# A graph network on one core: where the 0/1 matrices of destination lanes are made

## The reference

```
out0 = segment_sum(exp(-edge_weight) * x[src], dst)                  # layer 0
scores = einsum(Q[dst], K[src]) / 4 + edge_attr @ We.T + be          # layer 1, 4 heads
attn = softmax over the edges of a destination;  out = segment_sum(V[src] * attn, dst)
e = leaky_relu(x_l[src] + x_r[dst]) @ att; softmax; segment_sum      # layer 2, one head
h = relu((mean of neighbours + x) @ W1 + b1); the same with W2       # layer 3
```

## Time and profile before

| | us |
|---|---|
| median of three runs | 5168.92 |
| span of the profiled execution, first to last instruction | 3717.5 |
| VectorE busy | 2606.7 (70%) |
| TensorE busy | 2149.9 (58%) |
| POOL busy | 1984.6 (53%) |
| ScalarE busy | 796.1 (21%) |

### The profile page before, as it was taken

The page is one execution under the profiler, slowest core; times in us unless marked ns, Lnnn a source line. Parts: engine busy times, 40 slices in busy tenths (PEclk is TensorE's granted clock), DMA queues, the critical chain, the costliest instruction groups (busy, mean ns, idle before and its releaser), DMA issues. The chain is left out here.

```text
span 3717.5 us, 94213 instructions
## 1 busy us (share of the span) xinstructions
PE 2149.9 (58%) x24555; PEld 1628.6 (44%) x24556; DVE 2606.7 (70%) x5968; ACT 796.1 (21%) x2086; POOL 1984.6 (53%) x1987
## 2 busy tenths in 40 slices
PE   1435777566535555555655553465666666666597
PEld 0225666455534444444544442344444444444232
DVE  3898999888856777776777765477777777777511
ACT  0023555455520111111111110011111111111100
POOL 0112444333327777777777730777777777776000
PEclk9867889756655666666666665566666766666699
DMA  4046777788776667666666630565555555555687
GB/s 148 12 126 170 258 260 261 233 244 237 217 74 184 184 180 190 183 175 183 186 184 182 183 94 9 130 161 146 150 151 144 153 154 148 153 148 147 223 309 282
DMA packets 679457, 646.11 MB, mean 174 GB/s; under 512 B 129015, under 2 KB 513308, under 8 KB 678333
## 3 DMA queue, kind: packets, MB, share of 16 engines
q1 hardware_dynamic: 375773, 346.64, 31.7%
q0 software_dynamic: 77184, 154.07, 17.5%
q10 hardware_dynamic: 226300, 143.41, 12.6%
HBM read 433.64 MB, written 222.40 MB: 176 GB/s over the span
## 5 line engine op out<-in xcount | busy, mean ns | idle before, releaser
L1646 POOL DMA_INDIRECT rows<-nodes_xl,id_slot x832 | 831.1, 999 | 419.3 <-issue 249.5
L1646 POOL DMA_INDIRECT rows<-nodes_kv,id_slot x832 | 825.1, 992 | 290.8 <-issue 244.8
L1842 DVE SCALAR_TENSOR_TENSOR running_counts<-running_counts,same_block,counts_p 128x128 f32<-128x128 f32 x1144 | 393.9, 344 | 412.6 <-PE counts_p L2001 305.7
L2001 PE MATMUL counts_p<-hot_src,hot_blocks 128*128 128x128 bf16 x2288 | 291.9, 281 | 585.8 <-DVE running_counts L1842 584.4
L2001 PEld LDWEIGHTS counts_p<-hot_src,hot_blocks 128*128 128x128 bf16 x2288 | 217.6, 154 | 661.4 <-DVE running_counts L1842 599.4
L2045 PE MATMUL sums<-parts,hot 128*128 128x68 bf16 (+1 forms) x4992 | 325.2, 251 | 250.1 <-DVE parts L1826 250.1
L2045 PEld LDWEIGHTS sums<-parts,hot 128*128 128x128 bf16 x4992 | 311.6, 168 | 271.5 <-issue 271.5
L1091 POOL DMA_INDIRECT msg_by_src<-message,unit_slot x156 | 199.7, 1280 | 311.3 <-DVE message L944 292.4
L1260 PE MATMUL sums<-parts,hot 128*128 128x65 bf16 x3168 | 183.7, 235 | 120.7 <-DVE parts L1237 120.7
L1687 ACT CAST parts<-mixed 128x544 bf16<-128x544 f32 (+1 forms) x208 | 133.0, 639 | 536.1 <-DVE mixed L1810 278.1
L1971 PE MATMUL picked<-rows,ident 128*128 128x512 f32 x208 | 198.2, 1054 | 79.2 <-DMA rows<-nodes_xl,id_slot 68.3
(11 more groups left out here) (490 smaller groups left out, 4289.9 us busy)
## 6 DMA issues: line engine op xcount, KB each, us to landing
hot_src<-hot_src_by_cell SPq DMA_DIRECT2D x1144, 64.0 KB
adjacency<-running_counts ACTq DMA_DIRECT2D x1144, 64.0 KB
hotT<-hotT_by_step SPq DMA_DIRECT2D x208, 256.0 KB
hot<-hot_by_step SPq DMA_DIRECT2D x208, 256.0 KB
blocks<-adjacency SPq DMA_DIRECT2D x40, 1280.0 KB
hot_src_by_cell<-hot POOLq DMA_DIRECT2D x132, 256.0 KB
loc_all<-loc_by_cell SPq DMA_DIRECT2D x104, 256.0 KB
hotT_by_step<-hotT ACTq DMA_DIRECT2D x104, 256.0 KB
```

The costliest lines, as they stand in the source:

```text
L1646: pool.indirect_dma_start(out=rows[:, j, t, :], out_offset=None, in_=table, in_offset=bass.IndirectOffsetOnAxis(ap=ids[:, j, t:t + 1], axis=0)
L1842: v.scalar_tensor_tensor(runs[:, r, q, :], before_it, same[:, bass.ds(J * BBODY + (count_from + q), 1)], counts_p[:, q - HALVES[q >= len(H ...
L2001: ins = nc.tensor.matmul(counts_p[:, q - HALVES[half][0], :], hot_b[:, r, :, t], hot_s[:, r, q, :, g], start=g == 0, stop=g == 1)
```

## The change

`hot` and `hotT` are no longer made in the message stage, stored or loaded. In both attention loops SyncE loads the broadcast lane numbers (`loc_b`, 256 KB a step, ring of four) in the place of the `hotT` load; ScalarE makes `hotT` two steps ahead in two passes over 1024 columns, |lane - partition| and then relu(1 - that) (`lanes_hot`, right behind `next_ids`); VectorE makes `hot` of step J - 3 behind `hot_blocks` (`edges_hot`). The ids are made four steps ahead where it was two. The three bf16 parts of the sums stay.

```diff
--- messages: VectorE's build, ScalarE's store and SyncE's loads go
-                        v.tensor_scalar(hotT[:, q, :], loc_all[:, q, :], part[:], None, ALU.is_equal).then_inc(hotT_made, 1)
-                        v.tensor_tensor(
-                            hot[:, q, :, :], lane_h[:],
...
-                        act.dma_start(hotT_dram[bass.ds(J, 1), :, :].rearrange("a p e -> p (a e)"), hotT[:, q, :]).then_inc(hotT_kept[q], 16)
...
--- attend, SyncE
                             J = i * 8 + j
                             if not (isinstance(i, int) and J < 4):
-                                sp.wait_ge(products, J - 3)
-                            sp.dma_start(hotT[:, j % 4, :, :].rearrange("p t e -> p (t e)"),
-                                         hotT_dram[bass.ds(J, 1), :, :].rearrange("a p e -> p (a e)")).then_inc(hotT_in[j % 4], 16)
-                            if w is not None:
-                                hot_load(w, 1 - j // 4, j % 4)
+                                sp.wait_ge(away_made, J - 3)
+                            sp.dma_start(loc_b[:, j % 4, :], loc_flat[:, bass.ds(J * (TB * P), TB * P)].to_broadcast([P, TB * P])
+                                         ).then_inc(loc_in[j % 4], 16)
                             frm = several(block_cell[0:1, bass.ds(J * BBODY + count_from, BBODY)], EngineType.SP, CELLS_S)
                             if not (isinstance(i, int) and J < 2):
                                 sp.wait_ge(counted, (J - 1) * n_halves)
--- attend, ScalarE
+                        def lanes_hot(i, j):
+                            J = i * 8 + j
+                            act.wait_ge(minus_made, 1)
+                            act.wait_ge(loc_in[j % 4], (i * 2 + j // 4 + 1) * 16)
...
+                            nc.scalar.activation(away[:], loc_b[:, j % 4, :], ACT.Abs, bias=minus_part[:]).then_inc(away_made, 1)
+                            act.wait_ge(away_made, J + 1)
+                            if not (isinstance(i, int) and J < 4):
+                                act.wait_ge(products, J - 3)
+                            nc.scalar.activation(hotT[:, j % 4, :, :].rearrange("p t e -> p (t e)"), away[:], ACT.Relu, bias=1.0,
+                                                 scale=-1.0).then_inc(hotT_made, 1)
...
                             if live(i):
-                                next_ids(i, j + 2)
+                                next_ids(i, j + 4)
+                                ahead = (i, j + 2) if j < 6 else (i + 1, j - 6)
+                                if live(ahead[0]):
+                                    lanes_hot(*ahead)
--- attend, VectorE, behind hot_blocks
+                            if known_step(i, j - 3):
+                                edges_hot(i, j - 3)
```

More of the change, by code:

```diff
@@ L870, in _ @@
                 def _(sp):
-                    def loads(i):
-                        for q in range(NS):
-                            if not known(i, 1):
-                                sp.wait_ge(hotT_made, i * NS + q - (NS - 1))
-                            sp.dma_start(loc_all[:, q, :], loc_flat[:, bass.ds((i * NS + q) * (TB * P), TB * P)]
-                                         .to_broadcast([P, TB * P])).then_inc(loc_in[q], 16)
-                    loads(0)
                     later["load"](sp)
-                    loads(1)
                     later["keep_tables"](sp)
-                    loads(2)
-                    loads(3)
                     later["turn_stairs"](sp)
-                    with sp.Fori(4, ROUNDS) as i:
-                        loads(i)
                     later["all_kept"](sp)
@@ L894, in _ @@
                     step_own(v.tensor_copy(lane_u[:], lane[:].unsqueeze(2).to_broadcast([P, P, WT6])))
-                    step_own(v.tensor_copy(lane_h[:], lane[:].unsqueeze(2).to_broadcast([P, P, TB])))
                     step_own(v.memset(rows[:, :, :, D:D + 1], 1.0))
@@ L965, in step @@
                                 part_of(*at)
-                        if s in BUILD and inside(i):
-                            build(i, BUILD[s])
                     run(dve, step, lambda i: (later["tables"], later["links"], later["stairs"])[i](dve))
@@ L1076, in step @@
                                 part_of(*at)
-                        if s - 1 in BUILD and inside(i):
-                            store(i, BUILD[s - 1])
                     run(act, step)
-                    for q in range(NS):
-                        act.wait_ge(hot_kept[q], ROUNDS * 16)
-                        act.wait_ge(hotT_kept[q], ROUNDS * 16)
                 @block.gpsimd
@@ L1551, in attend, with run @@
                 n_halves = len(HALVES)
-                def run(eng, step):
+                def run(eng, step, peel=0):
                     for j in range(8):
                         step(0, j)
-                    with eng.Fori(1, LOOPS) as i:
+                    with eng.Fori(1, LOOPS - peel) as i:
+                        for j in range(8):
+                            step(i, j)
+                    for i in range(LOOPS - peel, LOOPS):
                         for j in range(8):
@@ L1663, in next_ids @@
                             nc.scalar.copy(ids[:, slot, :], gather_id[:, bass.ds(J * TB, TB)]).then_inc(ids_made, 1)
-                        next_ids(0, 0)
-                        next_ids(0, 1)
+                        for q in range(4):
+                            next_ids(0, q)
+                        nc.scalar.activation(minus_part[:], part[:], ACT.Copy, scale=-1.0).then_inc(minus_made, 1)
+                        def lanes_hot(i, j):
+                            J = i * 8 + j
+                            act.wait_ge(minus_made, 1)
+                            act.wait_ge(loc_in[j % 4], (i * 2 + j // 4 + 1) * 16)
+                            if not (isinstance(i, int) and J == 0):
+                                act.wait_ge(hotT_made, J)
+                            nc.scalar.activation(away[:], loc_b[:, j % 4, :], ACT.Abs, bias=minus_part[:]).then_inc(away_made, 1)
[4 more added lines that the diff above has]
+                                                 scale=-1.0).then_inc(hotT_made, 1)
+                        lanes_hot(0, 0)
+                        lanes_hot(0, 1)
                         def store(i, j):
@@ L1701, in step @@
                                 nc.scalar.activation(weight_T[0:R, :], gap[0:R, :], ACT.Exp, scale=-1.0).then_inc(exped, 1)
-                        run(act, step)
+                        run(act, step, peel=1)
                         for r in range(2):
```

72 lines of the change are left out of this document (27 added, 45 removed).

## The result

The changed kernel takes 5410.27 us (median of 4 runs, 5404.96 to 5414.84) beside 5166.26 us for the kernel before (4 runs): ratio 1.0475, 95% interval 1.0445 to 1.0505, or 244 us slower. Forecast were 5670 us and 505 us more.

The account below looks back on a forecast made before the run. VectorE bounds the message stage; in the loops no engine is full, POOL's gathers and a VectorE-TensorE-ScalarE chain being almost equally long. 354 + 229 - 78 = +505 us on 5168.9 gives 5674, say 5670 us; range 5260 to 5890.

Parts of the forecast that it names:

- I carry it as a constant: Whole run: the 1451.4 us between profiled span and median, unexplained by any row, was added unchanged to the forecast.
- the late load: Both loops: ScalarE stands at the lane numbers' load, issued behind SyncE's wait for counts; +354 and +229 us.
- The mechanism's own range: Whole run: bounds of landing, pair and message stage give 5446 to 5913 us; chance of this mechanism 0.80.
- Message stage: Message stage: without the matrices a step falls from 2.80 to 2.3 us, saving 78 us, bounds 108 and 47.
- Price of the pair: ScalarE in the loops: the two passes over 1024 columns take 2.4 us, at least 2.0, at most 3.2.
- Landing: Loops: the 256 KB lane numbers' load takes 3.5 us to land, bounds 2.0 and 4.7.
- First and second loop: Attention loops: 13.6 and 8.8 us more a window, times 26, so +354 and +229 us.
- VectorE's new instruction: Attention loops: 104 comparisons in each, hidden in the longer stalls, so 0; otherwise up to 47 and some 27 us.
- The sum: Whole kernel: 354 + 229 - 78 = +505 us, span from 3717.5 to about 4222 us.
- ScalarE is idle for four fifths of the span, so this alone hides: ScalarE in the loops: the two passes by themselves, without the wait for their load, cost no time.
- Rival 1: Loops: the load is not late, loops keep their period, the message stage's gain remains; 5085 us; chance 0.13.
- Rival 2: Loops: load not late, but VectorE's chain or POOL binds, 47 and some 27 us against 78; 5165 us; chance 0.07.

Follow-up runs that it names:

- the given trace: The profiled execution of the unchanged kernel before that the prediction used: span 3717.5 us, where the timed runs had a median of 5168.9 us.
- the kernel run again: The kernel before, unedited, timed and profiled once more: 5166.54 us, ratio 1.000, span 5169.4 us.
- 5236: The changed kernel with the lane numbers' load issued two steps earlier, ahead of SyncE's wait for the counts: 5236.18 us, ratio 1.0127.
- VectorE's half alone: The kernel before with `hot` made by VectorE in the loops; `hotT` still made in the message stage, stored and loaded: 5113.65 us, ratio 0.9899.

## Why the prediction was right in sign and wrong in size

**What failed** is the sentence "I carry it as a constant". The 1451.4 us were inside the span of every timed run, in the very loops for which I worked out the windows. A sum made of the given trace's windows could not be added to a median 39% above its span: in the timed runs a window takes 68.6 us (1783 / 26), in the given trace 41 to 42. The term that came out wrong by it is the late load. It stands at 583 us in the sum, and in the timed executions it measured 180 (beside ids four ahead, as in the change). The mechanism was right: ScalarE stands at that load for 2178 us, and with nothing due behind the pair the price is gone.

That 5410 lies between 5260 and 5890 is in part luck. The mechanism's own range, 5446 to 5913, doesn't hold it; only the room left for the unexplained 1451 us and for waits in the chains does.

**The steps, against runs without the stall** (two gathers of eight, where the kernel before takes what its given trace took):
- Message stage: -78 forecast, -107 measured (528.0 to 420.8 us between its first and last pick), at the edge of the bound of 108. The stage after was forecast rightly (2.3 us a step, 2.31 measured). The stage before was not: VectorE steps there in 3.03 us between 330 and 600 us, with two gathers and in the kernel run again, for 2.79 in the given trace. It waits 36 us for TensorE's picks there (7 in the given trace), and TensorE's granted clock was 0.77 between 400 and 550 us where the given trace has 0.86. That 494.6 less 416.5 makes 78 is luck: it sets one execution against another kind.
- Price of the pair: 2.4 forecast, 2.2 measured (1148 and 1057 ns). Landing: 3.5 forecast; 3.45 and 3.48 measured from issue to first pass, and a median of 3.8 to landing with the early load and two gathers.
- Late load in both loops: 583 forecast, 484 measured (4166.31 less 3682.70).
- First and second loop: +354 and +229 forecast. From first to last gather the kernel before with two gathers takes 1043.9 and 1061.6 us, the changed one 1350.0 and 1267.2: +306 and +206.
- VectorE's new instruction: 0 forecast, and beside the late load nothing says otherwise; without it, 25 us at most of the bound of 74.
- The sum: +505 forecast, +424 measured by the ratios (453 as the difference of the two times, which were taken beside different times of the kernel before).

**The same steps in the timed runs.** The first loop grew by 194 us (1976.5 for 1782.6), the second by 129, the message stage gave 115 by the time of the first gather, and 36 us came between the loops and behind them: 244. The late load is worth 180 us beside ids four ahead and 263 beside two (0.0348 and 0.0510), for 484 without the stall, although ScalarE stands longer at it (2178 us for 1160). That a window half as long again has slack in which part of each hold-up disappears fits this; I haven't traced which waits give it back.

**What I had not priced.** The ids four steps ahead: 175 us in the kernel before, nearly nothing beside the late load (0.0026), so they don't explain the miss. The given trace can't show their price, since POOL hardly paused there. And the pair in front of ScalarE's casts costs 0.028 (147 us) in the timed executions even when it waits for nothing: "ScalarE is idle for four fifths of the span, so this alone hides" is false there. Without the stall it nearly holds: the pair, VectorE's instruction and the ids come to 45 us together in both loops (1055.6 and 1094.9 us for 1043.9 and 1061.6). With ids four ahead the pair in front or last makes no such difference (1.0127 and 1.0175), so prices here do not add.

**The rivals.** Rival 1 (load not late) is excluded by the 2178 us; its number, 5085, would have needed more than an early load, as 5236 shows. Rival 2 is excluded by VectorE's half alone, whose loops pay 25 us and nothing for the 74 that it names.

## What to carry to other kernels

When the median lies far above the profiled span, find out first whether the trace is of the execution that is timed. Until then, a sum from its windows has an unknown size. A trial that doesn't get faster can still show that its cause was right: look whether the waits that it was to remove are gone, and what bounds the kernel now. An engine that is idle most of the time still sets the pace by the order of its queue: what is wanted two steps later goes behind what is wanted now. And the lead that a producer gets (ids two or four steps ahead) decides when DMAs come in bursts, so it needs a price of its own.

## What the runs showed of the hardware

- While POOL's gathers run in bursts of 16 (about 20 us, one in 1.25 us), TensorE falls to one matmul in 0.7 to 2.8 us with no releaser, mostly from 4 to 9 us into a burst until 1 to 4 us behind its end (the kernel run again, and with ids four ahead). Its signals come late in that time: VectorE and SyncE went on 13 us after the start of the last count that they waited for (1605.49, 1618.54). DMA issues stretch as well: five stores on ScalarE's queue took 6.39 us (2045.89, the changed kernel), the next five 2.33. With a quarter of the gathers the stall is gone, and with all of them, 2.12 us apart and each waited behind, it is gone too. What is starved the profile doesn't say.
- The same program ran once, in the given trace, with all its gathers, 1.297 us apart without a break, and without the stall. So the gathers' number and pace alone don't make it. What set that execution apart stays open.
- TensorE's granted clock was 0.595 over the span after, 0.604 in the kernel run again, and 0.677 with two gathers of eight (0.690 in the given trace). From first to last gather it averages 0.56 and 0.57 in the two loops of the kernel run again (0.64 and 0.67 in the given trace), mostly the lower level of 1.2 GHz. This is a small part of the 1450 us: TensorE is busy 1436.6 us in the two loops for 1278.2 in the given trace, 158 us more, while the loops grow by 1392. Nor does the lower clock make the gaps: with spaced gathers it is 0.58 in both loops, and they are gone.

The page "Runtime: NRT & Kernel Launch" of the Trainium skill, section "Instruction fetch mechanics", says that instructions arrive over a DMA queue in blocks of 256. A block that came late would leave one long gap ahead of many matmuls; the rows above show gaps of 0.4 to 2.6 us between single ones. So this rule alone doesn't explain them; and the profile's larger instruction queue moved the same 156 packets, 1.28 MB, with the stall and in the given trace. The page "ScalarE: Activation LUTs" of the Trainium skill, section "What ACT_TABLE_LOAD costs" (the prediction names the section behind it), gives 280 ns plus 0.833 ns a column with a pointer bias, 1133 ns for 1024, and 186 ns plus as much with immediate scale and bias, 1039 ns. The trace agrees: 1148 for the first pass, whose bias is a pointer, and 1057 for the second. With the overlap of 93 ns that the page states, the pair would be some 2.1 us, an estimate from these figures, where the prediction has 2.3; 2.14 was measured.
